# A four-stage transformer kernel: both halves of each batch's product of probabilities and values issued together, at the place of the second half

## The chip, the cores and the metric

The kernel runs on one core of one Trainium2 chip. The metric is the device time of one launch in microseconds (us). Engines are called by their names or as the profile writes them: TensorE (PE for its matmuls, PEld for its weight loads), VectorE (DVE), ScalarE (ACT), GpSimd (POOL), and SyncE (SP), which issues most of the DMAs.

## The reference

The input is `x` of 32 batches x 128 tokens x 144 channels, and a condition of 144 numbers per batch. Three transformer layers follow one another, then a rotation. What the change touches is the attention of each layer, with 16 heads of 9 channels:

```python
ada = silu(c) @ W_ada + b_ada          # shift, scale and gate for attention and for the MLP
h = modulate(layernorm(x), shift_msa, scale_msa)
q, k, v = split(h @ W_qkv + b_qkv)     # 16 heads of 9 channels each
attn = softmax(q @ k.T * 9 ** -0.5)    # 128 x 128 per head
o = (attn @ v).reshape(b, l, 144)
x = x + gate_msa * (o @ W_proj + b_proj)
```

After it each layer has an MLP: dense in layers 0 and 2, four experts with the best two of them per token in layer 1. The last stage rotates 64 directions of every token by the exponential of a skew matrix made from the condition.

## The kernel before

Everything stays in SBUF; each engine has one queue of instructions, written out by hand, and engines wait for one another by semaphores. What stands in an engine's queue behind a waiting instruction waits too, so the order written in the code is the order of the work.

Attention goes over 32 batches in pairs: `pair(i)` exists for TensorE, VectorE and ScalarE, and each call of it issues the steps of the even batch `e = 2i` and the odd batch `o = 2i + 1`, interleaved with later steps of the batches before and with the projection of the pair after. For one batch the steps are these:

- `turn` (L1541, L1542) transposes the normalised tokens, ScalarE modulates them (L1193, L1195), `qkv_product` (L1527) makes queries, keys and values, `qk_turned` (L1569) transposes queries and keys, and ScalarE copies them to `Q` and `KK` (L1235). Before that VectorE makes the low parts of queries and keys (L577), and ScalarE a doubled copy (L1228).
- `scores(b1, b2, a)` does two things in turns of one matmul each: scores of batch `b1`, half `a` of its heads (L1584, into `PSA`), from which VectorE takes the maximum over the keys (`row_max`, L582); and transposed scores of batch `b2` (L1591, into `PSB`), from which ScalarE makes the probabilities (`exps`, L1245) in `PT`. Both halves' maxima are transposed by `max_turn` (L1619), and VectorE adds them to the queries (`max_row`, L590), so that the second scores come out with the maximum taken off. `scores(., b2, 0)` waits for `max_row` of `b2` (the semaphore `mrow`).
- `pv(b, u, a)` (L1608) is the product of probabilities and values of one half of the heads: 8 matmuls of 32 output columns, in the trace 16 passes, into one half of the bank `PS6`. `a = 1` comes first, `a = 0` second. The first waits until the bank has been copied out for the batch before (`ot_ev`) and for the probabilities of its half, the second for the probabilities of the other half. Only the second signals `pv_done`.
- ScalarE copies the bank out (`out_copy`, L1251), `out_back` (L1629) transposes it, VectorE divides by the sums (`inverse_sums` L599, `normalise_out` L604), `out_turn` (L1634, L1635) transposes back, ScalarE copies (L1257, L1258), `project` (L1639, L1640) projects, and VectorE gates (L554), adds (L559) and takes statistics (L562).

In TensorE's `pair(i)` the two halves of a batch's `pv` stand apart, each between other work. The queue of one pair, in order: `pv(e-2, 1)`, `out_turn(e-4)`, `scores(e, o-2, 0)`, `pv(e-2, 0)`, two `qk_turned` with `project(e-4)` between them, `scores(e, o-2, 1)`, `qkv_product(i+1, 0)`, `out_back(o-4)`, `pv(o-2, 1)`, `max_turn(e)`, `out_turn(o-4)`, `qk_turned(i+1, 0)`, `scores(o, e, 0)`, `project(o-4)`, `qk_turned(i+1, 1)`, `turn(i+2)`, `scores(o, e, 1)`, `pv(o-2, 0)`, `out_back(e-2)`, `qkv_product(i+1, 1)`, `max_turn(o)`. A `passage` takes the last batches of a layer into the MLP; it issues `pv` of the last two batches itself.

VectorE has extra work in some pairs: small steps of the deviation in the second and the twelfth pair of a layer, and the low parts of the MLP's weights (`mlp_split`) after the fourth to the seventh. ScalarE casts these weights (`mlp_cast`) after the third to the sixth. GpSimd works through all of attention on a chain of its own, an orthogonalisation.

Of the kernel before, what the change touches and what calls it, by code (L numbers as in the profile page):

```python
# [47 lines left out]
def wait(eng, sem, value):  # L48

    if isinstance(value, int) and value <= 0:  # L50
        return
    eng.wait_ge(sem, value)
# [7 lines left out]
def program(nc, d, out, gates_dram, skew_dram):  # L60
    ctx = ExitStack()
    with ctx:
# [1408 lines left out]
        def _(pe):  # L1471
# [32 lines left out]
            def keep_warm(bank, n):  # L1504

                for _ in range(n):
                    mm(bank[:, 0:256], ident, K[:, 0:256], start=True, stop=True)
# [22 lines left out]
            def attention(l):  # L1530
# [28 lines left out]
                def qk_turned(P, j):  # L1559

                    pn, s = NP * l + P, j // 2
                    pe.wait_ge(qk_lo, 2 * pn + s + 1)
                    pe.wait_ge(qk_dup, 2 * pn + s + 1)
                    if j == 1 or j == 2:
                        pe.wait_ge(qk_rd, 4 * pn + j)
                    elif j == 3:
                        pe.wait_ge(mrow, NB * l + 2 * P) if P else pe.wait_ge(hf_ready, n_h(l, 0) + 2)
                    for g in range(G):
                        last = nc.tensor.transpose(turn_bank(pn, j)[:, g * 128:(g + 1) * 128],  # L1569
                                                   qt[:, s, j % 2, 4 * g:4 * g + 4, :].rearrange("p h w -> p (h w)").bitcast(F32), ident)  # L1570
                    last.then_inc(qk_turn, 1)

                def scores(b1, b2, a):

                    if b1 is not None:
                        wait(pe, max_done, 2 * (NB * l + b1) + a)
                    if b2 is not None:
                        pe.wait_ge(mrow, NB * l + b2 + 1)
                        wait(pe, exp_done, 2 * (NB * l + b2) + a)
                    for g in range(G):  # L1580
                        for r in range(2):
                            if b1 is not None:
                                rows, q0, par = slice(HP * (2 * a + r), HP * (2 * a + r + 1)), (b1 % 2) * 128, b1 // 2 % 2
                                one = mm(PS[r][:, g * 128:(g + 1) * 128], Q[rows, par, g, q0:q0 + 128],  # L1584
                                         KK[rows, par, g, q0:q0 + 128], start=True, stop=True)
                                if g == G - 1 and r == 1:
                                    one.then_inc(s1_done, 1)
                            if b2 is not None:
                                c = 1 - a
                                rows, q0, par = slice(HP * (2 * c + r), HP * (2 * c + r + 1)), (b2 % 2) * 128, b2 // 2 % 2  # L1590
                                two = mm(PS[2 + r][:, g * 128:(g + 1) * 128], KK[rows, par, g, q0:q0 + 128],  # L1591
                                         Q[rows, par, g, q0:q0 + 128], start=True, stop=True)
                                if g == G - 1 and r == 1:
                                    two.then_inc(s2_done, 1)

                def pv(b, u, a):

                    n = NB * l + b
                    if n == 0:
                        pe.wait_ge(s_gev, 1)  # L1600
                    if a == 1:
                        wait(pe, ot_ev, n)
                        pe.wait_ge(v_ev, n + 1)
                    pe.wait_ge(exp_done, 2 * n + 2 - a)
                    for g in range(G):
                        for r in range(2):
                            p0, at = HP * (2 * (g % 2) + r), a * 128
                            last = mm(PS[6][p0:p0 + HP, at:at + 128], VA[:, u, G * g + 2 * a + r, :],  # L1608
                                      PT[:, u % 2, a, (G * r + g) * 128:(G * r + g + 1) * 128], start=(g < 2), stop=(g >= 2))
                    if a == 0:  # L1610
                        last.then_inc(pv_done, 1)
# [20 lines left out]
                def out_turn(b, u):  # L1632
                    pe.wait_ge(norm_done, NB * l + b + 1)
                    nc.tensor.transpose(tail_bank(b)[:, 0:128], oq[:, u % 2, 0:C0], ident)  # L1634
                    nc.tensor.transpose(tail_bank(b)[0:C1, 128:256], oq[:, u % 2, C0:C + 1], ident).then_inc(ot2_done, 1)  # L1635

                def project(b, u):
                    pe.wait_ge(oT_ev, NB * l + b + 1)
                    mm(tail_bank(b)[:, 0:C], oT[:, u % 2, 0:128], wp0[:, l % 2, :], start=True, stop=False)  # L1639
                    mm(tail_bank(b)[:, 0:C], oT[:, u % 2, 128:256], wp1[:, l % 2, :], start=False, stop=True).then_inc(y_done, 1)  # L1640

                def pair(i):

                    def at(lag):
                        return 0 <= i - lag < NB // 2

                    e, o = 2 * i, 2 * i + 1
                    now = at(0)
                    before = 0 <= o - 2 < NB
                    if at(1):  # L1650
                        pv(e - 2, (e - 2) % 4, 1)
                    if at(2):
                        out_turn(e - 4, e % 2)
                    if now:
                        pe.wait_ge(qk_rd, 4 * (NP * l + i) + 2)
                    scores(e if now else None, o - 2 if before else None, 0)
                    if at(1):
                        pv(e - 2, (e - 2) % 4, 0)
                    if i == 0:
                        keep_warm(PS[2], 3)  # L1660
                    if now:
                        qk_turned(i, 2)
                    if at(2):
                        project(e - 4, e % 2)
                    if now:
                        qk_turned(i, 3)
                    if i == 0 and l == 0:
                        keep_warm(PS[2], 5)
                    scores(e if now else None, o - 2 if before else None, 1)
                    if at(-1):  # L1670
                        qkv_product(i + 1, 0)
                    elif i == NP - 1:
                        pe.wait_ge(qk_rd, 4 * (NP * l + i) + 3)
                        keep_warm(PS[4], 3)
                    if 0 <= o - 4 < NB:
                        out_back(o - 4, o % 2)
                    if before:
                        pv(o - 2, (o - 2) % 4, 1)
                    if now:
                        max_turn(e)  # L1680
                    if 0 <= o - 4 < NB:
                        out_turn(o - 4, o % 2)
                    if i == 0:
                        keep_warm(PS[2], 2)
                    if at(-1):
                        qk_turned(i + 1, 0)
                    elif i == NP - 1:
                        keep_warm(PS[4], 2)
                    if now:
                        pe.wait_ge(qk_rd, 4 * (NP * l + i + 1))  # L1690
                        scores(o, e, 0)
                    if 0 <= o - 4 < NB:
                        project(o - 4, o % 2)
                    if at(-1):
                        qk_turned(i + 1, 1)
                    elif i == NP - 1:
                        keep_warm(PS[4], 2)
                    if 0 <= i + 2 < NL:
                        turn(i + 2, i % 2)
                    if now:  # L1700
                        scores(o, e, 1)
                    if before:
                        pv(o - 2, (o - 2) % 4, 0)
                    if at(1):
                        out_back(e - 2, e % 2)
                    if at(-1):
                        qkv_product(i + 1, 1)
                    elif i == NP - 1:
                        keep_warm(PS[4], 3)
                    if now:  # L1710
                        max_turn(o)

                def passage(first, turn_rows):
# [27 lines left out]
                    if l != 1:  # L1741
                        turn_rows(2, 0)

                return pair, turn, qkv_product, qk_turned, passage

            def mlp(l, nxt):
# [488 lines left out]
```

## Time and profile before

| | us |
|---|---|
| runs | 1230.32, 1230.67, 1232.1; median 1230.67 |
| profiled execution, its own time | 1235.86 |
| its span, first to last instruction | 1234.1 |
| TensorE busy (matmuls) | 1173.2 (95%) |
| VectorE busy | 928.6 (75%) |
| ScalarE busy | 787.4 (64%) |
| GpSimd busy | 741.4 (60%) |

Busy time is the union of an engine's instructions; on TensorE matmuls overlap, and a busy TensorE is not one at its peak. A start in the timeline is when an instruction began, the number after it how long it lasted, and a number in brackets how long the engine had stood idle before it and what ended that. `issue` there means that nothing in the profile shows what the engine waited for. A `pv` block is 16 passes in one row. An instruction can start before the one ahead of it has ended, so on TensorE the distance between two starts says what an instruction costs those behind it. Attention takes three stretches: about 36 to 233, 340 to 540 and 896 to 1100 us.

### The profile page before, as it was taken

The page shows a single profiled execution, that of the slowest core. Times are in us where ns is not written, and L with a number is a line of the kernel's source. Part 1 is how long each engine was busy: PE and PEld are TensorE (multiplying, and loading weights), DVE is VectorE, ACT ScalarE, POOL GpSimd, SP SyncE. Part 2 cuts the span into 40 slices and gives each one's busy share as a digit, 9 for nine tenths or more (in the row PEclk, how much of TensorE's full clock was granted, in tenths as well). Part 3 has the DMA queues.
Part 4 walks back from the last instruction along what each step waited for, and adds up shares of the span by engine and source line. Part 5 has one row for each costly group of instructions (what it writes and reads, how often), then busy time and mean ns, then how long its engine had stood idle before and what let it go on. Part 6 is the DMA issues. An engine that isn't in the chain of part 4 may idle for free.

```text
span 1234.1 us, 35426 instructions
## 1 busy us (share of the span) xinstructions
PE 1173.2 (95%) x12826; PEld 938.0 (76%) x12826; DVE 928.6 (75%) x2503; ACT 787.4 (64%) x1809; POOL 741.4 (60%) x2055
## 2 busy tenths in 40 slices
PE   5899999999999999999999999999979999999997
PEld 3677777788767777778887888888857777777886
DVE  6899999776479999975667556656599999976532
ACT  3589888766578988873432442342468888876551
POOL 5566566566656666565667666666888888870000
PEclk8899999999979999999999999999989999999999
DMA  6322212342451211222111202111120111100121
GB/s 176 64 16 18 23 17 21 47 100 30 86 100 16 20 18 18 20 45 40 23 13 31 33 4 33 32 14 42 52 61 31 34 34 32 35 11 12 28 47 51
DMA packets 59408, 47.09 MB, mean 38 GB/s; under 512 B 9223, under 2 KB 54842, under 8 KB 58805
## 3 DMA queue, kind: packets, MB, share of 16 engines
q1 hardware_dynamic: 54972, 34.18, 12.2%
q0 software_dynamic: 3488, 8.52, 9.3%
q10 hardware_dynamic: 780, 2.17, 0.5%
q8 instruction: 104, 1.70, 0.5%
q14 instruction: 64, 0.52, 0.2%
HBM read 38.06 MB, written 3.10 MB: 33 GB/s over the span
## 4 chain that ended last, share of the span: by engine, by line
PE 79%; DVE 15%; issue 4%; ACT 2%; DMA 0%; SPq 0%; DVEq 0%; ACTq 0%
PE PS L1826 15%; PE PSA L1527 15%; PE PS L1608 7%; PE PSA L1584 7%; PE PS L1569 6%; PE PS L1527 6%; DVE BIG L582 4%; PE PSB L1794 2%; PE PS L1639 2%; PE PS L1629 2%; PE PS L1640 1%; PE PS L1843 1%; PE PS L1619 1%; PE PS L1634 1%; PE PSB L1591 1%
## 5 line engine op out<-in xcount | busy, mean ns | idle before, releaser
L1378 ACT ACTIVATE BIG<-PSA 128x512 f32<-128x512 f32 (+1 forms) x224 | 132.4, 595 | 248.7 <-PE PSA L1527 248.6
L582 DVE TENSOR_REDUCE BIG<-PSA 128x8 f32<-128x1024 f32 x192 | 234.2, 1220 | 26.3 <-PE PSA L1584 25.0
L1826 PE MATMUL PS<-w,BIG 128*128 128x144 f32 (+1 forms) x1664 | 223.4, 287 | 1.8 <-DVE BIG L866 1.3
L1826 PEld LDWEIGHTS PS<-w,BIG 128*128 128x128 f32 (+1 forms) x1664 | 213.6, 190 | 9.3 <-DVE BIG L866 2.2
L1245 ACT ACTIVATE BIG<-PSB 128x1024 f32<-128x1024 f32 x192 | 195.8, 1020 | 19.8 <-PE PSB L1591 19.4
L1584 PEld LDWEIGHTS PSA<-KK,Q 32*128 32x128 f32 x1536 | 105.4, 189 | 60.0 <-issue 38.7
L1584 PE MATMUL PSA<-KK,Q 32*128 32x128 f32 x1536 | 130.1, 286 | 18.0 <-DVE BIG L582 6.8
L2071 POOL MEMSET qrows<- 128x2 f32 x63 | 6.2, 99 | 209.5 <-DMA VB<-qrows 209.5
L1591 PE MATMUL PSB<-Q,KK 32*128 32x128 f32 x1536 | 130.0, 287 | 0.0
L1569 PE MATMUL PS<-K,qt 128*128 128x128 f32 x768 | 123.3, 286 | 6.7 <-issue 3.1
L1608 PE MATMUL PS<-BIG,VA 128*32 128x128 f32 x3072 | 126.7, 284 | 1.6 <-DVE col L457 1.6
L1569 PEld LDWEIGHTS PS<-K,qt 128*128 128x128 f32 x768 | 88.9, 144 | 30.1 <-issue 15.6
L1591 PEld LDWEIGHTS PSB<-Q,KK 32*128 32x128 f32 x1536 | 102.8, 189 | 1.1 <-DVE Q L590 0.6
L1527 PE MATMUL PSA<-hhi,Mhi 128*128 128x512 f32 (+1 forms) x224 | 100.0, 446 | 1.5 <-ACT BIG L1378 1.0
L1608 PEld LDWEIGHTS PS<-BIG,VA 128*32 128x32 f32 x3072 | 73.7, 111 | 30.1 <-issue 21.1
L2056 POOL TENSOR_TENSOR QU<-qtree 128x72 f32<-128x72 f32 (+5 forms) x288 | 82.0, 285 | 22.5
L1527 PE MATMUL PSA<-hhi,Mlo 128*128 128x512 f32 (+1 forms) x224 | 88.5, 395 | 0.0
L1527 PE MATMUL PSA<-h,MW 128*128 128x512 f32 (+1 forms) x224 | 88.4, 395 | 0.0
L1527 PE MATMUL PSA<-hlo,Mhi 128*128 128x512 f32 (+1 forms) x224 | 87.9, 392 | 0.0
L2056 POOL TENSOR_TENSOR qtree<-QU 128x36 f32<-128x36 f32 (+5 forms) x288 | 68.6, 238 | 22.6
L866 DVE SCALAR_TENSOR_TENSOR BIG<-PS,BIG 128x144 f32<-128x144 f32 x96 | 34.9, 366 | 56.3 <-PE PS L1826 56.1
L1220 ACT ACTIVATE qt<-PS 128x288 fp32r<-128x288 f32 x93 | 41.4, 445 | 56.1 <-PE PS L1527 56.0
(330 smaller groups left out, 3066.1 us busy)
## 6 DMA issues: line engine op xcount, KB each, us to landing
gate<-gates SPq DMA_DIRECT2D x96, 72.0 KB, 2.9
mgate<-gates SPq DMA_DIRECT2D x96, 72.0 KB, 2.8
VB<-skew POOLq DMA_DIRECT2D x16, 288.0 KB, 3.7
Q<-skew SPq DMA_DIRECT2D x32, 128.0 KB, 3.0
X<-in_x SPq DMA_DIRECT2D x4, 576.0 KB, 10.0
out<-X SPq DMA_DIRECT2D x8, 288.0 KB, 3.6
BIG<-in_skew_w SPq DMA_DIRECT2D x2, 1024.0 KB
BIG<-in_wqkv SPq DMA_DIRECT2D x2, 584.0 KB
```

Source lines behind the costliest of these rows:

```text
L582: V.tensor_reduce(nmax.rearrange("p (s w) -> p s w", w=HP)[:, 2 * a:2 * a + 2, 3 * HD:3 * HD + G], PSA[:, :].rearrange("p (r g k) -> p r g ...
L866: V.scalar_tensor_tensor(a, ps, cw[:, s * NE + e:s * NE + e + 1], a, ALU.mult, ALU.add).then_inc(acc_done, 1)
L1220: S.activation(qt[:, s, :, :, 0:HD], src, ACT.Copy).then_inc(qk_hi, 1)
L1245: S.activation(PT[:, u % 2, a, :], PSB[:, :], ACT.Exp, scale=float(HD) ** -0.5).then_inc(exp_done, 1)
L1378: S.activation(hm[0:rows, slot, :], PS[(par * FTOT[l] + j) % 2][0:rows, :], gelu).then_inc(gelu_done, 1)
L1527: last = mm(o, a, b, start=(k == 0), stop=(k == 3))
L1569: last = nc.tensor.transpose(turn_bank(pn, j)[:, g * 128:(g + 1) * 128], qt[:, s, j % 2, 4 * g:4 * g + 4, :].rearrange("p h w -> p (h w)") ...
L1584: one = mm(PS[r][:, g * 128:(g + 1) * 128], Q[rows, par, g, q0:q0 + 128], KK[rows, par, g, q0:q0 + 128], start=True, stop=True)
L1591: two = mm(PS[2 + r][:, g * 128:(g + 1) * 128], KK[rows, par, g, q0:q0 + 128], Q[rows, par, g, q0:q0 + 128], start=True, stop=True)
L1608: last = mm(PS[6][p0:p0 + HP, at:at + 128], VA[:, u, G * g + 2 * a + r, :], PT[:, u % 2, a, (G * r + g) * 128:(G * r + g + 1) * 128], star ...
L1826: last = mm(o, hm[0:rows, slot, s * 128:(s + 1) * 128], w2[0:rows, w0 + k, :], start=(k == 0), stop=(k == tiles - 1))
L2056: link(R.tensor_tensor(t, a[:, :, 0:size], a[:, :, size:2 * size], ALU.add))
```

## The change

In TensorE's `pair(i)` the first half of `pv` is taken from its two places and put directly ahead of the second half, for the even and for the odd batch. No wait, matmul, bank or operand changes, and VectorE's and ScalarE's queues are the same.

```diff
@@ def pair(i), TensorE @@
                     before = 0 <= o - 2 < NB
-                    if at(1):
-                        pv(e - 2, (e - 2) % 4, 1)
                     if at(2):
                         out_turn(e - 4, e % 2)
                     if now:
                         pe.wait_ge(qk_rd, 4 * (NP * l + i) + 2)
                     scores(e if now else None, o - 2 if before else None, 0)
                     if at(1):
-                        pv(e - 2, (e - 2) % 4, 0)
+                        for a in (1, 0):
+                            pv(e - 2, (e - 2) % 4, a)
...
                     if 0 <= o - 4 < NB:
                         out_back(o - 4, o % 2)
-                    if before:
-                        pv(o - 2, (o - 2) % 4, 1)
                     if now:
                         max_turn(e)
...
                     if now:
                         scores(o, e, 1)
                     if before:
-                        pv(o - 2, (o - 2) % 4, 0)
+                        for a in (1, 0):
+                            pv(o - 2, (o - 2) % 4, a)
```

TensorE's order from the end of `scores(o, e, 1)` to the start of the next pair's `scores(e, o-2, 0)`, in an ordinary pair of layer 0. Each row is an instruction with its line, its output and inputs (PS6 is the bank of `pv`, PS5 that of the max transpose, PS7 that of the projection) and how many follow one another. Before:

```order
L1591 MATMUL PSB<-Q,KK 128x128
L1608 MATMUL PS6<-BIG,VA 32x128 x8
L1629 MATMUL PS7<-K,BIG 128x128 x2
L1527 MATMUL PS4<-Ahi,hhi 128x432
L1527 MATMUL PS4<-Alo,hhi 128x432
L1527 MATMUL PS4<-Ahi,hlo 128x432
L1527 MATMUL PS4<-AW3,h3 128x432
L1619 MATMUL PS5<-K,BIG 128x128
L1608 MATMUL PS6<-BIG,VA 32x128 x8
L1634 MATMUL PS7<-K,BIG 128x128
L1635 MATMUL PS7<-K,BIG 17x128
L1584 MATMUL PSA<-KK,Q 128x128
```

And in the change:

```order
L1591 MATMUL PSB<-Q,KK 128x128
L1608 MATMUL PS6<-BIG,VA 32x128 x16
L1629 MATMUL PS7<-K,BIG 128x128 x2
L1527 MATMUL PS4<-Ahi,hhi 128x432
L1527 MATMUL PS4<-Alo,hhi 128x432
L1527 MATMUL PS4<-Ahi,hlo 128x432
L1527 MATMUL PS4<-AW3,h3 128x432
L1619 MATMUL PS5<-K,BIG 128x128
L1634 MATMUL PS7<-K,BIG 128x128
L1635 MATMUL PS7<-K,BIG 17x128
L1584 MATMUL PSA<-KK,Q 128x128
```

The block of the odd batch has 16 matmuls in place of 8, ahead of the max transpose L1619, and the 8 of the even batch behind that transpose are gone.

TensorE's order behind the first `scores` of a pair, before:

```order
L1591 MATMUL PSB<-Q,KK 128x128
L1608 MATMUL PS6<-BIG,VA 32x128 x8
L1569 MATMUL PS4<-K,qt 128x128 x4
L1639 MATMUL PS7<-wp0,BIG 128x144
L1640 MATMUL PS7<-wp1,BIG 128x144
L1569 MATMUL PS5<-K,qt 128x128 x4
L1584 MATMUL PSA<-KK,Q 128x128
```

And in the change:

```order
L1591 MATMUL PSB<-Q,KK 128x128
L1608 MATMUL PS6<-BIG,VA 32x128 x16
L1569 MATMUL PS4<-K,qt 128x128 x4
L1639 MATMUL PS7<-wp0,BIG 128x144
L1640 MATMUL PS7<-wp1,BIG 128x144
L1569 MATMUL PS5<-K,qt 128x128 x4
L1584 MATMUL PSA<-KK,Q 128x128
```

Here too 8 matmuls became 16, between the pair's first `scores` and its second.

TensorE's order around the third place, in the middle of the pair, before:

```order
L1527 MATMUL PS4<-AW3,h3 128x432
L1629 MATMUL PS7<-K,BIG 128x128 x2
L1608 MATMUL PS6<-BIG,VA 32x128 x8
L1619 MATMUL PS5<-K,BIG 128x128
L1634 MATMUL PS7<-K,BIG 128x128
L1635 MATMUL PS7<-K,BIG 17x128
L1569 MATMUL PS4<-K,qt 128x128 x4
```

And in the change:

```order
L1527 MATMUL PS4<-AW3,h3 128x432
L1629 MATMUL PS7<-K,BIG 128x128 x2
L1619 MATMUL PS5<-K,BIG 128x128
L1634 MATMUL PS7<-K,BIG 128x128
L1635 MATMUL PS7<-K,BIG 17x128
L1569 MATMUL PS4<-K,qt 128x128 x4
```

The 8 matmuls of the odd batch's first half, ahead of the max transpose of the even batch, are gone from here.

## Rows read from the trace of the kernel before

**Rows 1.** The page: span, busy time by engine, and the chain by engine.

```profile
span 1234.1 us, 35426 instructions
...
PE 1173.2 (95%) x12826; PEld 938.0 (76%) x12826; DVE 928.6 (75%) x2503; ACT 787.4 (64%) x1809; POOL 741.4 (60%) x2055
...
PE 79%; DVE 15%; issue 4%; ACT 2%; DMA 0%; SPq 0%; DVEq 0%; ACTq 0%
```

**Rows 2.** Groups by line: `pv`; busy us, mean ns of one | idle before, releaser.

```profile
L1608 PE MATMUL PS<-BIG,VA 128*32 128x128 f32 x3072 | 126.7, 284 | 1.6 <-DVE col L457 1.6
```

**Rows 3.** Timeline, TensorE, scores(o, ., 1) to the next pair: start us, us, instruction.

```profile
219.72 0.32 PE L1584 MATMUL PSA<-KK,Q 32*128 32x128 f32 x1
...
220.11 0.27 PE L1584 MATMUL PSA<-KK,Q 32*128 32x128 f32 x1
...
220.31 0.65 PE L1608 MATMUL PS<-BIG,VA 128*32 128x128 f32 x16
220.89 0.44 PE L1629 MATMUL PS<-K,BIG 128*128 128x128 f32 x2
...
221.96 0.27 PE L1619 MATMUL PS<-K,BIG 128*128 128x128 f32 x1
222.16 0.64 PE L1608 MATMUL PS<-BIG,VA 128*32 128x128 f32 x16
222.73 0.33 PE L1634 MATMUL PS<-K,BIG 128*128 128x128 f32 x1
222.90 0.27 PE L1635 MATMUL PS<-K,BIG 128*17 128x128 f32 x1
223.21 0.29 PE L1584 MATMUL PSA<-KK,Q 32*128 32x128 f32 x1
```

**Rows 4.** Timeline, VectorE, the same stretch.

```profile
221.85 0.31 DVE L604 TENSOR_TENSOR BIG<-PS,BIG 128x144 f32<-128x144 f32 x1
222.26 0.69 DVE L590 TENSOR_TENSOR Q<-Q,PS 128x512 fp32r<-128x512 f32 x1
```

**Rows 5.** Timeline, TensorE, from the pair's first scores to its second.

```profile
211.08 0.29 PE L1584 MATMUL PSA<-KK,Q 32*128 32x128 f32 x1
...
211.68 0.64 PE L1608 MATMUL PS<-BIG,VA 128*32 128x128 f32 x16
212.25 0.65 PE L1569 MATMUL PS<-K,qt 128*128 128x128 f32 x4
...
213.77 0.32 PE L1584 MATMUL PSA<-KK,Q 32*128 32x128 f32 x1
```

**Rows 6.** Timeline, TensorE, the middle of the pair.

```profile
215.57 0.64 PE L1608 MATMUL PS<-BIG,VA 128*32 128x128 f32 x16
216.15 0.33 PE L1619 MATMUL PS<-K,BIG 128*128 128x128 f32 x1
...
216.76 0.66 PE L1569 MATMUL PS<-K,qt 128*128 128x128 f32 x4
217.56 0.29 PE L1584 MATMUL PSA<-KK,Q 32*128 32x128 f32 x1
```

**Rows 7.** Timeline, VectorE, the middle of the pair; in brackets idle before, releaser.

```profile
214.48 1.23 DVE L582 TENSOR_REDUCE BIG<-PSA 128x8 f32<-128x1024 f32 x1 [0.52 <-PE PSA L1584]
...
216.20 0.51 DVE L577 TENSOR_TENSOR qt<-PS,qt 128x144 fp32r<-128x144 f32 x2
216.62 0.68 DVE L590 TENSOR_TENSOR Q<-Q,PS 128x512 fp32r<-128x512 f32 x1
```

**Rows 8.** Timeline, TensorE, three waits in pairs of layers 1, 1 and 2.

```profile
407.23 0.63 PE L1569 MATMUL PS<-K,qt 128*128 128x128 f32 x4 [0.77 <-issue]
...
434.87 0.32 PE L1584 MATMUL PSA<-KK,Q 32*128 32x128 f32 x1 [0.47 <-DVE BIG L582]
...
924.71 0.29 PE L1584 MATMUL PSA<-KK,Q 32*128 32x128 f32 x1 [0.22 <-DVE Q L590]
```

**Rows 9.** Timeline, ScalarE, the copy after the projection.

```profile
215.46 0.45 ACT L1220 ACTIVATE qt<-PS 128x288 fp32r<-128x288 f32 x1 [0.98 <-PE PS L1527]
```

## The prediction

> **What bounds the kernel now.** I read, in this order: the page, the groups of instructions, then TensorE's and VectorE's timeline through one ordinary pair of batches. The page shows TensorE 95% busy and 79% of the chain on it, VectorE 75% and 15% [rows 1]. That looks like a kernel bound by TensorE, so that what a stage gains or loses there would be gained or lost in full. The timeline says more: in attention the chain passes from TensorE to VectorE and back four times a pair, and only some of TensorE's work lies on it.
>
> Take the pair from 211.08 to 223.21, 12.13 us [rows 3, 5]. Its four blocks of L1608 are called here A (even batch, first half, 222.16), B (even, second half, 211.68), C (odd, first half, 215.57) and D (odd, second half, 220.31). The change takes away A and C and doubles B and D.
>
> - Both `scores(., ., 0)` start 0.26 us after an L590 ends: 222.26 + 0.69 = 222.95 against 223.21, and 216.62 + 0.68 = 217.30 against 217.56 [rows 3, 4, 6, 7]. The distance is 0.24 to 0.26 in nearly all the pairs, whatever TensorE did before; where TensorE stands idle longer, the row itself names L590, as at 924.71 [rows 8]. So these two starts are VectorE's. At 222.95 + 0.26 TensorE has nothing to say.
> - From `scores(e, ., 0)` (211.08) to `scores(e, ., 1)` (213.77) TensorE runs without a wait, B in the middle, and VectorE then stands idle 0.52 us for it before its L582 [rows 5, 7]. B is on the path.
> - From that L582 (214.48) VectorE runs in one piece to L590 (216.62) [rows 7]. L590 needs the max transpose, L1619 at 216.15 + 0.33 = 216.48: ready 0.14 us early. C, which stands ahead of L1619, is off the path.
> - From `scores(o, ., 1)` (219.72) D, L1629, the projection and L1619 (221.96) follow without a gap, and L590 starts at 222.26, 0.03 after L1619's end (222.23), while VectorE was done with L604 at 222.16 [rows 3, 4]. D is on the path. A comes after that L1619 and ends before 223.21: off the path.
>
> **The change, part by part.** Nothing is added or taken away in sum: 3072 passes of L1608 [rows 2] stay 3072, and VectorE's and ScalarE's orders are the same. 15 pairs a layer have all four blocks (the last two batches go through the passage, unchanged), so 45 pairs in all.
>
> *B and D grow.* A block's 16 passes last 0.65 from the first start to the last end, of which the last pass is 0.27 (the mean of [rows 2] is 284 ns, most are 273): 15 steps in 0.38, or 25 ns each. 16 more cost 16 x 0.025 = 0.40 us. The exit after the block (0.20) is there as before.
>
> *D*: L1619 goes from 221.96 to 222.36, L590 from 222.26 to 222.66, the next `scores(e, ., 0)` from 223.21 to 223.61. VectorE's other way there gives no relief: L1629 is also 0.40 later, ends at 221.73, then L599 and L604 end at about 222.35, before 222.66. In full: 45 x 0.40 = 18.0. In three pairs (the twelfth of layers 0 and 2, the second of layer 2) small VectorE steps (the deviations) stand before L590 and cover 0.14 to 0.24: -0.6. D: +17.4 us.
>
> *B*: the same 0.40 on `scores(e, ., 1)`, and VectorE is idle there already, so it is passed on. But here other waits cover it in part of the pairs, which I went through one by one in both timelines by the starts of L1584 and L582; the three kinds that matter most have a row each. Full 0.40 in 25 pairs: 10.0. In 6 pairs of layers 0 and 2 the distance from `scores(e, ., 0)` to `scores(e, ., 1)` is 2.77 in place of 2.69, which covers 0.09: 6 x 0.31 = 1.9. In 5 pairs VectorE covers 0.1 to 0.37: together 1.0 left. In 9 pairs it costs nothing: in the second pairs of the three layers and the twelfth of layer 2, where VectorE is late by more; in four pairs of layer 1, where TensorE waits 0.77 behind B for ScalarE, which casts weights there (407.23), and in the one after them, where L582 ends 0.47 late (434.87) [rows 8]. B: +12.9 us. If those covers were gone the whole 18.0 would be due.
>
> *C goes.* TensorE reaches L1619 about 0.6 sooner and waits there for L582 to end (214.48 + 1.23 = 215.71). L590 stays VectorE's. What is late next is L582 itself. Only in the last pair of a layer, where L590 waits 0.23 for L1619, is that gained: 3 x 0.23 = -0.7. Nothing else moves up: L1634 waits for L604, and L1569 at 216.76 for L577 (216.20 + 0.51) [rows 6, 7].
>
> *A goes.* TensorE runs from L1619 straight to L1634 and then waits for L590, some 0.7 us idle in place of A's 0.57 and a little more. Gain 0. The first half now waits for nothing new: its probabilities and the emptied bank were ready a quarter of a pair earlier. ScalarE's copy L1251 gets its second-half signal later by 0.40, at D some 0.1 after ScalarE is free for it; ScalarE has 0.98 idle a pair before its L1220 [rows 9].
>
> Sum: 17.4 + 12.9 - 0.7 = **+29.6 us**. Against the profiled execution (1234.1 span, 1235.86 time) that is 1265.5; against the median of the three runs, 5.2 below it, 1230.67 + 29.6 = **1260.3 us**, +2.4%.
>
> The one price not in a row is the step between passes where one half follows the other. The nearest is the step within a block, 25 ns (0.40 a block). From below: if the second half needed no steps of its own but overlapped, 0; from above, as if it were a block of its own with entry and exit, 0.57, which gives 0.57/0.40 x 30.3 - 0.7 = +42. I take 25 ns, since the second half has the same shapes and the same order of column strips as the first; neither end has a row for it.
>
> **A rule against this forecast.** In the rows a block of L1608 costs 0.20 to get in (220.11 to 220.31) and 0.20 to get out, beside 0.38 of passes: 0.58 from its first pass to the next work, 220.31 to 220.89 [rows 3]. The Trainium skill, "TensorEngine Tiling (Array Packing)", Key Properties, says that changing the tiling mode, not just the tile, drains the engine. Blocks of 32-column tiles beside full-array transposes are such changes, and the change halves them. The trace agrees that a switch costs some 0.1 to 0.2 us. What all of them together would give is the first rival, -18 us, against +29.6 by the sum above; I keep the sum, since A's and C's switches lie where TensorE waits anyway.
>
> **The rivals.**
>
> *Fewer switches pay (faster).* If TensorE set the pace everywhere, A's place would shrink from 0.77 (221.96 to 222.73) to 0.17, the spacing of two full transposes (222.73 to 222.90) [rows 3], and C's alike: 2 x 0.60 - 2 x 0.40 = 0.40 us a pair, 45 x 0.40 = 18: 1212.7. It decides where `scores(., ., 0)` is TensorE's and not L590's. For it: TensorE's 95%. Against it: the 0.26 behind L590 in both places. Chance 0.08.
>
> *Half the cost.* Something I haven't seen covers B or D throughout, as ScalarE covers B in four pairs: without B +17.4 - 0.7 = +16.7, 1247.4, and without D +12.9 - 0.7 = +12.2, 1242.9. For it: many near ties (0.1 to 0.2 us) around L582 and L590. Against: VectorE's 0.52 idle in front of L582. Chance 0.15.
>
> *All of it.* The covers also move, and 2 x 45 x 0.40 = 36 is paid: 1266.7, a little more if ScalarE falls behind by its later L1251. Chance 0.13.
>
> *Nothing.* The later blocks go into VectorE's waiting time and the pair stays at 12.13. VectorE has 0.5 idle a pair, but all of it ahead of the very L582 that B would delay. Chance 0.05.
>
> That the change doesn't do what it says can be set aside: TensorE's order shows 16 in one row where 8 and 8 stood.
>
> **How the numbers follow.** The forecast has 0.59. A measurement of this kernel tells about 0.2% (2.5 us) from no change. Slower by over 0.2%: 0.59 + 0.15 + 0.13 = 0.87; same 0.05; faster 0.08. The range, 1243 to 1268, takes in the forecast, half the cost and nearly all of the case with all of it: 0.85 less what sizes may be off, about 8 in 10. The far ends of the unknown step (+42, 0) stay outside.
>
> **What would show it.** In the profile after: an ordinary pair of 12.9 us; L1608 in blocks of 32; `scores(e, ., 1)` 3.09 behind `scores(e, ., 0)`; L590 of the odd batch 2.94 behind `scores(o, ., 1)` (now 2.54); VectorE idle 0.9 before the L582 of 214.48; `scores(., ., 0)` still 0.26 behind L590, now with TensorE idle before it and L590 as releaser; L1619 of the even batch waiting for L582. In layer 1's pairs with weight casts the wait before L1569 shrinks from 0.77 to about 0.37. Wrong would be: a pair of 12.1 or less, or a `scores(., ., 0)` that starts well over 0.26 behind L590.

## The result, and the profile after

| | before | after |
|---|---|---|
| runs, us | 1229.3, 1230.32, 1230.67, 1232.1 | 1266.55, 1266.92, 1270.06, 1273.39 |
| median, us | 1230.49 | 1268.49 |
| ratio, 95% interval | | 1.0303 [1.0274, 1.0332] |
| profiled execution, its own time / span | 1235.86 / 1234.1 | 1266.92 / 1265.1 |
| TensorE busy | 1173.2 (95%) | 1164.2 (92%) |
| mean granted clock of the profiled execution | 0.985 | 0.981 |

The change makes the kernel slower by 38.0 us in the medians, 3%. The forecast was +29.6 us, 1260.3, with a range up to 1268.0: the direction and most of the size are as forecast, but the median lies 0.5 us above the top of the range.

The page after, to be held against [rows 1]: the same instructions, a TensorE that is busy for 9 us less in a span 31 us longer, and a chain with a little less TensorE and more VectorE in it.

```profile
span 1265.1 us, 35426 instructions
...
PE 1164.2 (92%) x12826; PEld 947.3 (75%) x12826; DVE 932.4 (74%) x2503; ACT 797.0 (63%) x1809; POOL 744.3 (59%) x2055
...
PE 77%; DVE 17%; issue 4%; ACT 2%; DMA 0%; SPq 0%; DVEq 0%; ACTq 0%
```

The groups after, with their idle time and what ended it; `pv` is the row that answers to [rows 2].

```profile
L1608 PE MATMUL PS<-BIG,VA 128*32 128x128 f32 x3072 | 107.0, 279 | 0.0
L1584 PE MATMUL PSA<-KK,Q 32*128 32x128 f32 x1536 | 131.0, 287 | 47.1 <-DVE Q L590 34.0 <-DVE BIG L582 3.3 <-ACT BIG L1245 2.5
L582 DVE TENSOR_REDUCE BIG<-PSA 128x8 f32<-128x1024 f32 x192 | 234.3, 1220 | 40.5 <-PE PSA L1584 39.1
L590 DVE TENSOR_TENSOR Q<-Q,PS 128x512 fp32r<-128x512 f32 x96 | 65.6, 683 | 15.5 <-PE PS L1619 15.3
```

And the same last three groups before.

```profile
L1584 PE MATMUL PSA<-KK,Q 32*128 32x128 f32 x1536 | 130.1, 286 | 18.0 <-DVE BIG L582 6.8 <-ACT BIG L1245 2.4 <-DVE Q L590 1.3
L582 DVE TENSOR_REDUCE BIG<-PSA 128x8 f32<-128x1024 f32 x192 | 234.2, 1220 | 26.3 <-PE PSA L1584 25.0
L590 DVE TENSOR_TENSOR Q<-Q,PS 128x512 fp32r<-128x512 f32 x96 | 65.6, 683 | 8.5 <-PE PS L1619 4.7
```

`pv` itself is cheaper: two blocks of 16 were busy 0.65 each, one of 32 is busy 1.08, and 90 x 0.22 is the 20 us by which its busy time falls. The kernel is slower all the same. TensorE now stands idle 34.0 us for L590 in place of 1.3: that is where A and C used to be. VectorE waits 14.1 us more for the scores (B) and 10.6 us more for the max transpose (D).

TensorE's timeline of an ordinary pair (layer 1, start 458.01, next pair 471.01), to be held against [rows 3, 5, 6]. Start us, length us, instruction, and in brackets idle before and releaser.

```profile
458.01 0.29 PE L1584 MATMUL PSA<-KK,Q 32*128 32x128 f32 x1 [0.75 <-DVE Q L590]
...
458.61 1.08 PE L1608 MATMUL PS<-BIG,VA 128*32 128x128 f32 x32
459.62 0.66 PE L1569 MATMUL PS<-K,qt 128*128 128x128 f32 x4
...
461.13 0.32 PE L1584 MATMUL PSA<-KK,Q 32*128 32x128 f32 x1
...
463.13 0.33 PE L1619 MATMUL PS<-K,BIG 128*128 128x128 f32 x1
...
464.92 0.29 PE L1584 MATMUL PSA<-KK,Q 32*128 32x128 f32 x1
...
467.08 0.32 PE L1584 MATMUL PSA<-KK,Q 32*128 32x128 f32 x1
...
467.68 1.08 PE L1608 MATMUL PS<-BIG,VA 128*32 128x128 f32 x32
468.69 0.44 PE L1629 MATMUL PS<-K,BIG 128*128 128x128 f32 x2
...
469.76 0.27 PE L1619 MATMUL PS<-K,BIG 128*128 128x128 f32 x1
...
471.01 0.29 PE L1584 MATMUL PSA<-KK,Q 32*128 32x128 f32 x1 [0.76 <-DVE Q L590]
```

VectorE's timeline of the same pair, to be held against [rows 4, 7].

```profile
461.85 1.23 DVE L582 TENSOR_REDUCE BIG<-PSA 128x8 f32<-128x1024 f32 x1 [0.73 <-PE PSA L1584]
...
463.99 0.68 DVE L590 TENSOR_TENSOR Q<-Q,PS 128x512 fp32r<-128x512 f32 x1
...
470.06 0.69 DVE L590 TENSOR_TENSOR Q<-Q,PS 128x512 fp32r<-128x512 f32 x1 [0.30 <-PE PS L1619]
```

The pair takes 13.00 us, 0.87 more than the 12.13 of [rows 3, 5]. Both steps lie where they were looked for: from the pair's first scores to its second 3.12 (461.13 - 458.01) in place of 2.69, and from the odd batch's second scores to its L590 2.98 (470.06 - 467.08) in place of 2.54. From a block's first pass to the work behind it is 1.01 (468.69 - 467.68) in place of 0.58, so a doubled block costs 0.43.

**By stretches.** The starts of the first L582 of each pair cut attention into stretches. In the two profiled executions, us:

| | layer 0 | layer 1 | layer 2 |
|---|---|---|---|
| first two pairs, before / after | 28.28 / 27.63 | 27.75 / 28.96 | 29.00 / 32.13 |
| next 13 pairs, before / after | 160.50 / 170.59 | 164.28 / 172.28 | 163.45 / 172.27 |

The 39 pairs of the second row grow by 26.9 together, and everything outside the table by 0.4. The other 3.7 are in the first pairs of the layers, where the granted clock comes in.

Cut by the starts of the scores, the same 39 pairs show where the growth lies. From a pair's first scores to its second (B) they grow by 13.1 in all, and from the odd batch's second scores to the next pair's first (D) by 16.6, together 29.7. The two stretches between shrink by 3.2. Nearly all of that (2.8 net) is single waits of 0.2 to 1.0 us between the odd batch's first and second scores, which the profile before has and the profile after lacks; `e10_project_late`, which leaves `pv` as it was, lacks 1.3 of them too. They look like differences between executions and not like the change; their cause was not followed.

**The clock.** Windows where it was lowest, of the profile after and then of the profile before: us, busy time and instructions of PE, PEld, DVE, ACT and POOL, then the granted clock, DMA share and GB/s.

```profile
365.00:370.00 5.00, 4.42 (x28) 3.29 (x26) 2.02 (x9) 2.21 (x6) 2.40 (x6) 0.50 0.43 26
935.00:940.00 5.00, 4.12 (x29) 3.02 (x28) 4.25 (x15) 3.49 (x7) 3.85 (x12) 0.50 0.00 0
```

```profile
350.00:355.00 5.00, 5.00 (x56) 3.49 (x55) 3.29 (x9) 3.22 (x7) 2.97 (x8) 0.50 0.80 155
355.00:360.00 5.00, 5.00 (x43) 3.56 (x41) 3.04 (x12) 2.52 (x7) 2.64 (x10) 0.50 0.20 21
```

In both kernels TensorE runs at 1.2 GHz in part of the first pairs of the layers and at 2.4 GHz in the pairs after them. How much of it is at 1.2 GHz differs between runs of one and the same kernel: 54 undisturbed runs of the kernel before, beside these experiments, lie between 1239.6 us (mean granted clock 0.981) and 1227.11 (0.993), and only 2 of them were granted 0.981 or less. A straight line through them loses 0.73 us per 0.001 of clock and leaves a scatter of 1.4 us. The four runs of the change were granted 0.979, 0.981, 0.981 and 0.987 (median 0.981), against a median of 0.990. Measured from the line at its own clock, the change costs 32.5 us in the mean of the four (29.5 to 34.5). The other 5.5 of the 38.0 go with the clock. "At equal clock" below always means this line.

### The profile page after: what moved, and what is told of

Read it like the earlier page. It is cut to its first block, busy times and chain, and to the rows that moved or that the text cites. A ratio compares the mean times of both kernels' runs of the same rounds, so it can differ in the third digit from the quotient of the medians.

```text
span 1265.1 us, 35426 instructions
## 1 busy us (share of the span) xinstructions
PE 1164.2 (92%) x12826; PEld 947.3 (75%) x12826; DVE 932.4 (74%) x2503; ACT 797.0 (63%) x1809; POOL 744.3 (59%) x2055
## 4 chain that ended last, share of the span: by engine, by line
PE 77%; DVE 17%; issue 4%; ACT 2%; DMA 0%; SPq 0%; DVEq 0%; ACTq 0%
PE PSA L1527 15%; PE PS L1824 15%; PE PSA L1584 8%; PE PS L1608 7%; PE PS L1569 7%; DVE BIG L582 6%; PE PS L1527 3%; DVE Q L590 2%; PE PSB L1792 2%; PE PS L1639 2%; PE PS L1640 2%; PE PS L1629 1%; PE PSB L1591 1%; PE PS L1841 1%; PE PS L1507 1%
## 5 line engine op out<-in xcount | busy, mean ns | idle before, releaser
L582 DVE TENSOR_REDUCE BIG<-PSA 128x8 f32<-128x1024 f32 x192 | 234.3, 1220 | 40.5 <-PE PSA L1584 39.1
L1569 PE MATMUL PS<-K,qt 128*128 128x128 f32 x768 | 126.0, 291 | 5.6 <-DVE qt L577 4.0
L1569 PEld LDWEIGHTS PS<-K,qt 128*128 128x128 f32 x768 | 91.0, 147 | 29.5 <-DVE qt L577 16.2
L1608 PE MATMUL PS<-BIG,VA 128*32 128x128 f32 x3072 | 107.0, 279 | 0.0
L1608 PEld LDWEIGHTS PS<-BIG,VA 128*32 128x32 f32 x3072 | 78.9, 111 | 8.8 <-issue 2.0
L2054 POOL TENSOR_TENSOR qtree<-QU 128x36 f32<-128x36 f32 (+5 forms) x288 | 71.6, 248 | 22.6
L1235 ACT ACTIVATE Q<-PS 128x512 fp32r<-128x512 f32 x96 | 56.5, 589 | 38.6 <-PE PS L1569 37.5
L590 DVE TENSOR_TENSOR Q<-Q,PS 128x512 fp32r<-128x512 f32 x96 | 65.6, 683 | 15.5 <-PE PS L1619 15.3
```

What stands on the lines that cost most here:

```text
L582: V.tensor_reduce(nmax.rearrange("p (s w) -> p s w", w=HP)[:, 2 * a:2 * a + 2, 3 * HD:3 * HD + G], PSA[:, :].rearrange("p (r g k) -> p r g ...
L590: V.tensor_tensor(q, q.bitcast(F32), PS[5][:, 0:128].rearrange("p (o n) -> p o n", o=1).broadcast_to([128, G, 128]), ALU.add).then_inc(mro ...
L1235: S.activation((Q, KK)[j % 2][:, pn % 2, :, s * 128:(s + 1) * 128], turn_bank(pn, j)[:, :].rearrange("p (g n) -> p g n", g=G), ACT.Copy).t ...
L2054: link(R.tensor_tensor(t, a[:, :, 0:size], a[:, :, size:2 * size], ALU.add))
```

## The experiments

The theory: what a `pv` half costs depends on where it stands. At B and D TensorE is on the path and the half costs its passes; at A and C TensorE waits for VectorE and the half costs nothing. The rivals: TensorE's total sets the pace (then leaving halves out anywhere gains, and fewer blocks gain), or keeping the halves together is bad in itself.

**Each batch alone.** `e1_odd_merged` changes the odd batches alone (C goes, D doubles), `e2_even_merged` the even ones (A goes, B doubles).

```diff
@@ e1_odd_merged @@
-                    if before:
-                        pv(o - 2, (o - 2) % 4, 1)
                     if now:
                         max_turn(e)
...
                     if before:
-                        pv(o - 2, (o - 2) % 4, 0)
+                        for a in (1, 0):
+                            pv(o - 2, (o - 2) % 4, a)
@@ e2_even_merged @@
-                    if at(1):
-                        pv(e - 2, (e - 2) % 4, 1)
...
                     if at(1):
-                        pv(e - 2, (e - 2) % 4, 0)
+                        for a in (1, 0):
+                            pv(e - 2, (e - 2) % 4, a)
```

> Only the odd batch's halves together (C gone, D doubled). Path theory: each D grows by 0.43 us (what the doubled block shows in the profile after), 45 x 0.43 = +19 us, less 0.7 for the last pairs: +18 to +20. If the two merges share the loss evenly: +19 as well, so it is the pair with the next run that tells. If TensorE's total were the bound: 45 x (0.43 - 0.60) = -8.

> Only the even batch's halves together (A gone, B doubled). Path theory with covers: 0.43 in full in some 25 pairs, in part or not at all in the other 20: +12 to +15, clearly less than the run with the odd batch. Even sharing: +19. If TensorE's total were the bound: -8.

Measured: odd alone 1257.25 us, ratio 1.0193 [1.0140, 1.0246]; even alone 1246.72, ratio 1.0111 [1.0075, 1.0146], before 1231.95. At equal clock that is +19.3 and +14.2. The two add up to 33.5, against 32.5 for the change, which is within the scatter: the parts are independent, and neither "half the cost" nor a common cause is needed. D is the dearer one, as forecast.

**Halves left out.** `e3_first_left_out` takes A and C out altogether, in every pair from the third on; the second half takes over their waits. Half of the product of probabilities and values is not computed there.

```diff
-                def pv(b, u, a):
+                def pv(b, u, a, only=False):
...
-                    if a == 1:
+                    if a == 1 or only:
...
-                    if at(1):
+                    if at(1) and i == 1:
                         pv(e - 2, (e - 2) % 4, 1)
...
-                        pv(e - 2, (e - 2) % 4, 0)
+                        pv(e - 2, (e - 2) % 4, 0, i > 1)
...
-                    if before:
+                    if before and i == 1:
                         pv(o - 2, (o - 2) % 4, 1)
...
-                        pv(o - 2, (o - 2) % 4, 0)
+                        pv(o - 2, (o - 2) % 4, 0, i > 1)
```

> The first halves A and C are left out in all but the second pair of a layer (42 pairs of 45), nothing is put in their place, so half of the product of probabilities and values of these batches is not computed; the waits stay, at the second half. Path theory: A and C lie where TensorE waits for VectorE, so 0 to -2 us (0.23 in each layer's last pair). If TensorE's total were the bound: 42 x 1.2 = -50.

Measured: 1234.37, ratio 1.0013 [0.9984, 1.0042]; at equal clock 0.0. TensorE does 1344 passes fewer, and the time doesn't move. Its timeline at A's place shows why:

```profile
147.16 0.27 PE L1619 MATMUL PS<-K,BIG 128*128 128x128 f32 x1
147.47 0.69 DVE L590 TENSOR_TENSOR Q<-Q,PS 128x512 fp32r<-128x512 f32 x1
148.42 0.29 PE L1584 MATMUL PSA<-KK,Q 32*128 32x128 f32 x1 [0.55 <-DVE Q L590]
```

The scores start 0.26 behind the end of L590 (148.16), as before; A's place has turned into idle time. This also answers the rule on tiling modes: with A and C their entries and exits are gone too, and nothing is gained. By that rule (the Trainium skill, "TensorEngine Tiling (Array Packing)", Key Properties) TensorE was to save the drains of the switches that go. The trace agrees as to TensorE (a block of 32 has 1.01 where two of 16 had 2 x 0.58); but this was not on the path.

**The same growth with nothing taken away.** `e4_odd_second_twice` issues D's matmuls twice, `e8_odd_first_twice` C's, both where they stand before; the product is formed twice from the same operands, with the same result.

```diff
-                def pv(b, u, a):
+                def pv(b, u, a, times=1):
...
-                    for g in range(G):
+                    for g in [g for _ in range(times) for g in range(G)]:
...
@@ e4_odd_second_twice @@
-                        pv(o - 2, (o - 2) % 4, 0)
+                        pv(o - 2, (o - 2) % 4, 0, 2)
@@ e8_odd_first_twice @@
-                        pv(o - 2, (o - 2) % 4, 1)
+                        pv(o - 2, (o - 2) % 4, 1, 2)
```

> D's matmuls are issued twice (the same result written again), A, B and C stay. Path theory: the loss comes from what is added at D, whether or not C is taken away: +18 to +20, the same as with the odd batch's halves together. If taking C away had given something back that hid a larger loss: above +24. If the second half's own waits were the cost and not its passes: 0, since the doubled matmuls wait for nothing.

> C's matmuls are issued twice in place, nothing else. Path theory: C is off the path with 0.14 to spare before L590 (L1619 ends at 216.48, L590 starts at 216.62), so 0.43 - 0.14 = 0.29 a pair, some 40 pairs: +10 to +13, less than the +17 of the same passes at D. If C were as far off the path as A's and C's removal alone would suggest: 0.

Measured: D twice 1248.62, ratio 1.0143 [1.0100, 1.0187], +18.7 at equal clock, within the scatter of the +19.3 of e1. So D's growth alone gives the odd batch's whole loss, and what C's removal does is nothing that these runs can tell from scatter. C twice: 1246.15, ratio 1.0147 [1.0082, 1.0212], +14.9 at equal clock, above the 10 to 13 expected. C is off the path by a margin only, and the margin is 0.10 and not 0.14: by [rows 6, 7] L1619 was ready 0.14 before L590, but when L1619 is what L590 waits for, L590 starts 0.04 behind its end (156.61 against 156.24 + 0.33). A second block brings 0.43, in the trace an ordinary pair is 0.33 longer between its second scores and the odd batch's first, and 45 x 0.33 = 14.9. The timeline of e8, with L1619 now as the releaser of an L590 that had no wait in [rows 7]:

```profile
155.23 1.08 PE L1608 MATMUL PS<-BIG,VA 128*32 128x128 f32 x32
155.85 0.51 DVE L577 TENSOR_TENSOR qt<-PS,qt 128x144 fp32r<-128x144 f32 x2
156.24 0.33 PE L1619 MATMUL PS<-K,BIG 128*128 128x128 f32 x1
156.61 0.69 DVE L590 TENSOR_TENSOR Q<-Q,PS 128x512 fp32r<-128x512 f32 x1 [0.24 <-PE PS L1619]
```

**Together, but at the other place.** `e5_even_at_first` keeps the even batch's halves together too, at A's place.

```diff
                     if at(1):
-                        pv(e - 2, (e - 2) % 4, 1)
+                        for a in (1, 0):
+                            pv(e - 2, (e - 2) % 4, a)
...
-                    if at(1):
-                        pv(e - 2, (e - 2) % 4, 0)
```

> The even batch's halves together at the place of the first (A doubled, B gone), odd batch as before. Path theory: it is the place and not the togetherness that costs. TensorE reaches the next pair's first scores 0.43 later, but its way from there to the second scores is 0.57 shorter, down to what VectorE needs (L582 2.89 behind the first scores in place of 3.40, -0.51): -0.08 a pair, -4 us, between -6 and +2. If halves together cost as such: +13, as in the run with the even batch at the second place.

Measured: 1230.04, ratio 0.9985 [0.9958, 1.0012]; at equal clock -1.0. The same joining that costs 14 us at B costs nothing at A. So being together is not what hurts; the place is.

```profile
146.01 0.69 DVE L590 TENSOR_TENSOR Q<-Q,PS 128x512 fp32r<-128x512 f32 x1
...
147.28 0.32 PE L1584 MATMUL PSA<-KK,Q 32*128 32x128 f32 x1
...
149.39 0.32 PE L1584 MATMUL PSA<-KK,Q 32*128 32x128 f32 x1
```

The distance from the first to the second scores falls from 2.69 to 2.11 (149.39 - 147.28), but the first scores now start 0.58 behind L590's end (146.70) in place of 0.26: TensorE is late there by 0.32. More than half of the 0.58 gained is given back at once. Over the 39 pairs the way from the first to the second scores is 18.2 us shorter, the way to the next pair's first scores 12.6 longer, and the one from the second scores to the odd batch's first 3.9 longer, so 1.7 are left.

**Can the rest be had?** `e6_even_at_first_turn_late` also moves `out_turn(e-4)` behind the first scores; `e9_at_first_project_late` further moves `project(e-4)` behind the second `qk_turned`; `e10_project_late` is the kernel before with this last move alone.

```diff
@@ e6, e9 @@
                     if at(1):
-                        pv(e - 2, (e - 2) % 4, 1)
-                    if at(2):
-                        out_turn(e - 4, e % 2)
+                        for a in (1, 0):
+                            pv(e - 2, (e - 2) % 4, a)
...
                     scores(e if now else None, o - 2 if before else None, 0)
-                    if at(1):
-                        pv(e - 2, (e - 2) % 4, 0)
+                    if at(2):
+                        out_turn(e - 4, e % 2)
@@ e9, e10 @@
                         qk_turned(i, 2)
-                    if at(2):
-                        project(e - 4, e % 2)
                     if now:
                         qk_turned(i, 3)
+                    if at(2):
+                        project(e - 4, e % 2)
```

> As the run before it in this set, and the transposes L1634, L1635 of the even batch moved from ahead of the first scores to behind them, so that TensorE's last work before the first scores is the doubled A alone. Path theory: the first scores start by L590 again as in the kernel before, and the way to the second scores is 2.69 - 0.57 + 0.30 = 2.42: -0.27 a pair, -12 us, between -8 and -14, faster than before. If ScalarE's later copy L1257 (by 0.4) pushes its whole queue: -4 to +4.

> Even batch's halves together at the place of the first, its transposes L1634 and L1635 behind the first scores, and its projection behind the second L1569 instead of ahead of it. The run before with the transposes late lost 0.33 a pair (149.52 to 149.85) where the projection waited for ScalarE; now four transposes fill that time. Path theory: first to second scores 2.41 in place of 2.69, -0.26 a pair, 42 pairs: -11 us, between -7 and -13, so 1218 to 1224 at a clock of 0.99. If TensorE's other work only moves the wait elsewhere: -3 to +2.

> The kernel before with only the projection moved behind the second L1569. Path theory: TensorE has no wait there in an ordinary pair, so the distance between the scores stays 2.69 and the time too: -2 to +1 us. If the gain of the run before comes from the projection's place and not from the halves': the same gain here, -11.

Measured: e6 1231.82, ratio 1.0009 [0.9984, 1.0034], a miss; e9 1229.12, ratio 0.9985 [0.9972, 0.9998], of 11 us expected one or two; e10, ratio 1.0012 [0.9985, 1.0039], nothing. In e6 the gain ends in a new wait:

```profile
148.89 0.33 PE L1634 MATMUL PS<-K,BIG 128*128 128x128 f32 x1
149.37 0.28 ACT L1257 ACTIVATE BIG<-PS 128x128 f32<-128x128 f32 x1 [0.32 <-PE PS L1635]
149.85 0.51 PE L1639 MATMUL PS<-wp,BIG 128*128 128x144 f32 x2
```

`project` needs ScalarE's copy of the transposed output, and that copy can't begin before `out_turn`, so TensorE stands before L1639 and the first scores are 2.67 from the second, nearly the 2.69 of before. e9 removes this wait, but the distance falls to 2.55 only, by 0.14 in an ordinary pair where 0.28 was expected, and not at all in the pairs with other work in them. Why it stops there is open. e9 is the one version that beats the kernel before by more than its interval, by 0.15% and at the edge of it.

**The clock.** `e7_after_second_pair_apart` is the change, with the second pair of each layer left as before. In the profile of the change TensorE ran at 1.2 GHz in part of these pairs.

```diff
+                    if at(1) and i == 1:
+                        pv(e - 2, (e - 2) % 4, 1)
                     if at(2):
                         out_turn(e - 4, e % 2)
...
-                        for a in (1, 0):
+                        for a in ((0,) if i == 1 else (1, 0)):
                             pv(e - 2, (e - 2) % 4, a)
```

(Shown against the change; the odd batch alike.)

> The change, but the second pair of each layer as in the kernel before. Clock theory: the runs of the change have a mean granted clock of 0.979 to 0.987 where before mostly has 0.99, lost around the first pairs of the layers, and that is what the change lost beyond 32 us; if its second pair is the place, the clock comes back to about 0.99 and the time to 1259 to 1262. If the clock is lost for another reason: clock 0.982 as with the change, and 1266.

Measured: 1263.31, ratio 1.0262 [1.0204, 1.0321], its four runs granted 0.985 to 0.992. That is 5.2 us less than the change's median, and lies between the two expectations (up to 1262, or 1266). At equal clock it is +31.6, against +32.5 for the change: the three pairs' own saving of 1 to 3 us can't be told from scatter. The clock is higher, but the two sets of four overlap (0.979 to 0.987 and 0.985 to 0.992). And its profile doesn't bear out that the halves in the second pair are the place. Layer 2's second pair, left as before, is at 1.2 GHz for some 10 us here too, and takes 16.4 us in place of 13.3:

```profile
935.00:940.00 5.00, 5.00 (x44) 3.88 (x43) 2.74 (x9) 3.56 (x8) 4.08 (x13) 0.50 0.23 62
940.00:945.00 5.00, 4.44 (x56) 3.40 (x55) 3.50 (x6) 2.88 (x8) 4.29 (x11) 0.51 0.00 2
```

Of the twelve profiles the change, e1, e2 and e7, all with halves joined at the later place, have 7 to 14 us at 1.2 GHz in that pair, and the other eight none. So the change may well lower the clock there, but then not by the halves of that pair alone. With one profile of each this is a hint; whether the 5.5 us are the change's own doing stays open.

## Why the prediction was right, and where it was short

*What bounds.* Right. L590 sets both `scores(., ., 0)`, as the timelines of the pair show: 463.99 + 0.68 = 464.67 against 464.92, and 470.06 + 0.69 = 470.75 against 471.01, 0.25 and 0.26. TensorE has 0.76 idle before it there, with L590 as the releaser, as forecast.

*B and D, 0.40 each.* Right in place, short in size. A doubled block costs 0.43. The rows of one block, cut at later and later starts, show the step:

```profile
467.83 0.93 PE L1608 MATMUL PS<-BIG,VA 128*32 128x128 f32 x25
467.94 0.82 PE L1608 MATMUL PS<-BIG,VA 128*32 128x128 f32 x21
468.05 0.71 PE L1608 MATMUL PS<-BIG,VA 128*32 128x128 f32 x17
```

Four passes, one for each column strip, take 0.11 us, and a half is four such groups: 4 x 0.109 = 0.44. The single starts lie 7, 7, 6 and then 89 ns apart. The step that failed is "15 steps in 0.38, or 25 ns each". The 15 steps from a block's first start to its last leave out the long distance of the last group, which the exit covers in a block of 16 but which is paid in the middle of one of 32. Of the range for this unknown (0 to 0.57) the choice by the nearest row was the right one. The Trainium skill, "TensorE: Matmul & The Clock Gate", "Wait — 56ns, not 53.3ns?", states a floor of about 25 ns from start to start however few the columns; the trace has 27 in the mean and no such floor between single passes, of which three in four are 7 ns or less behind the one ahead, in other strips.

*How many pairs pay.* With 0.43 the sum of the prediction becomes D 45 x 0.43 - 0.6 = 18.8, B 25 x 0.43 + 6 x 0.34 + 1.2 = 14.0, and with C's -0.7 +32.1. The experiments gave +18.7 (e4) and +19.3 (e1) for D and +14.2 (e2) for B, and +32.5 for both. The covers of B that were counted pair by pair were real. In one kind of pair the account was wrong, though: in layer 1's four pairs with casts of weights D was to be paid in full. D's stretch is 0.44 longer there as elsewhere, but TensorE's wait ahead of L1569 shrinks further than to the 0.37 forecast, to 0.12:

```profile
405.19 1.08 PE L1608 MATMUL PS<-BIG,VA 128*32 128x128 f32 x32
406.39 0.63 PE L1569 MATMUL PS<-K,qt 128*128 128x128 f32 x4
```

(406.39 less 405.19 + 1.08.) The way from the first to the second scores is 0.19 to 0.22 shorter there than before, so the wait covers all of B and about 0.2 of D as well: some 0.8 us too much in the sum (4 x 0.2), which the totals can't show. Whether more of D is hidden there can't be read from the two profiles. Two such pairs, from the first L582 of one to that of the next, take 13.31 and 13.31 in place of 13.22 and 13.27, as if nearly all of it were; but the same two take 12.95 and 13.00 in e6, and 13.55 and 13.65 in e4, where D alone grew. That ScalarE's casts end this wait is argued from the order of the work; it was not tried.

*C and A go, 0.* Right, shown by e3 (they can be left out for nothing) and e4 (C's removal adds nothing to D's growth). The one gain that the sum had for C, 3 x 0.23 = -0.7 in the last pairs of the layers, did not come. These are the second scores of layer 0's last pair, L590 and the odd batch's first scores, before and then after:

```profile
226.07 0.32 PE L1584 MATMUL PSA<-KK,Q 32*128 32x128 f32 x1
...
229.32 0.69 DVE L590 TENSOR_TENSOR Q<-Q,PS 128x512 fp32r<-128x512 f32 x1 [0.23 <-PE PS L1619]
230.38 0.32 PE L1584 MATMUL PSA<-KK,Q 32*128 32x128 f32 x1
```

```profile
235.44 0.32 PE L1584 MATMUL PSA<-KK,Q 32*128 32x128 f32 x1
...
238.38 0.68 DVE L590 TENSOR_TENSOR Q<-Q,PS 128x512 fp32r<-128x512 f32 x1
...
239.75 0.32 PE L1584 MATMUL PSA<-KK,Q 32*128 32x128 f32 x1
```

L590 does lose its wait and starts 2.94 behind the second scores in place of 3.25. But the odd batch's first scores start 4.31 behind them in both. In this pair, unlike the others, they were 0.37 behind L590's end already before, so L590 was not what they waited for. The two slips of the sum, 0.7 gained by C that did not come and 0.8 too much in D, nearly cancel by luck: 18.8 + 14.0 - 0.8 = 32.0, against 32.5 measured.

*What would show it.* Blocks of 32; 3.09 from first to second scores (3.12); 2.94 to the odd L590 (2.98); a pair of 12.9 (13.00); L1619 of the even batch behind L582 (463.13, 0.05 after 461.85 + 1.23): these came out, each with the step's short measure in it. The 0.9 of idle time before L582 did not: it is 0.73. VectorE's L554 ahead of it waits for the projection, which stands behind B too, and takes the rest of the delay.

*The total.* +38.0 against +29.6. Of the 8.4 missing, 2.9 are there at equal clock (32.5 - 29.6), of which the mis-sized step gives 2.5 (18.8 + 14.0 in place of 17.4 + 12.9), and 5.5 go with the clock. No term of the sum was for the clock, and "all of it" at 1266.7 was reckoned as 36 us of passes: a number near the result for another reason. The first pairs of the layers run partly at 1.2 GHz, where a doubled block costs more as well:

```profile
941.76 1.94 PE L1608 MATMUL PS<-BIG,VA 128*32 128x128 f32 x32
```

Here 1.94 us in place of 1.08, in the second pair of layer 2. The range should have allowed for the clock: the profile before shows 0.50 in first and second pairs, and its mean clock of 0.985 stood in it. That the change itself lowers the clock is not shown.

*The rivals.* "Fewer switches pay" falls by e3; "nothing" falls by the pair; "half the cost" by e1 and e2, each of which has its own share; "all of it" is wrong in its reason, since B's covers stand (14.2 rather than 19.4).

## What to carry to other kernels

With an engine 95% busy, ask at each place whether its next wait would swallow the work: here 16 passes more cost 0.43 us at two places, while at two others they could be left out, 1344 in all, without a gain. No gain from leaving work out doesn't mean that more work is free: at C, 16 passes more used up a slack of 0.10 and cost 0.33. Read the slack from the start of the next instruction against the end of its other releaser (0.26 behind L590 while L590 is what it waits for, 0.58 in e5, where TensorE was late), not from the engine's idle time, of which there was none. When work is moved, size a step on a whole period of its pattern, since the first start to the last of a block leaves out one gap.

## What the runs showed of the hardware

- Most of the spread of this kernel goes with the clock: 1227.11 to 1239.6 us in 54 runs, 0.73 us per 0.001 of mean granted clock; about the line the scatter is 1.4 us, about the mean 2.7. Comparing runs at their own clock showed that e4 (+18.7) and e1 (+19.3) cost the same, which their medians (+16.7 and +25.3) hide, and that e1 and e2 add up to 33.5 against the change's 32.5; the medians alone (+25.3, +14.8 and +38.0) add up less well (40.1 against 38.0).
- Passes into the four column strips start 7, 7 and 6 ns apart, and the next group of four 89 ns later: 27 ns a pass in the mean, against 0.2 us for entering such a block and 0.2 for leaving it [rows 3]. A block of 32 in place of two of 16 has 1.01 in place of 1.16 us, so joining two such blocks saves 0.15 us of TensorE's time, which would show in the total only where TensorE is what is waited for; at A and C it is not (e3).
